# Setup of a gated cross-attention kernel: energies' input on 96 rows, other load order, gate transfers from ScalarE, Q ahead of K, first maxima between K and V

## The reference

```
xn     = layernorm(x)
Q,K,V  = xn @ Wq + bq, ctx @ Wk + bk, ctx @ Wv + bv        # 16 heads of 32
energy = mean(abs(ctxb), axis=-1);  energy /= max over keys + 1e-8
gate   = (energy > 0.1) * 0.9 + 0.1                        # one factor for each key
attn   = softmax(Q @ K.T / sqrt(32) * gate)
x      = x + tanh(g_xattn) * ((attn @ V) @ Wo + bo)
x      = x + tanh(g_ffn) * experts(layernorm(x))           # 2 shared, 16 routed, top 2
```

## Time and profile before

| what | us |
|---|---|
| median of 3 runs | 2094.84 (2093.85 to 2103.59) |
| the profiled execution | 2091.02 |
| its span | 2089.1 |
| TensorE busy in the span | 1935.3 (93%) |
| GpSimd busy | 1248.9 (60%) |
| VectorE busy | 1119.3 (54%) |
| ScalarE busy | 772.2 (37%) |
| TensorE's first matmul | 35.54 |
| first score of batch 0 | 76.36 |
| first matmul of batch 0's body | 99.76 |

### The profile page before, as it was taken

The page is one execution under the profiler, slowest core; times in us unless marked ns, Lnnn a source line. Parts: engine busy times, 40 slices in busy tenths (PEclk is TensorE's granted clock), DMA queues, the critical chain, the costliest instruction groups (busy, mean ns, idle before and its releaser), DMA issues. The chain is left out here.

```text
span 2089.1 us, 40601 instructions
## 1 busy us (share of the span) xinstructions
PE 1935.3 (93%) x12484; PEld 1503.2 (72%) x12485; DVE 1119.3 (54%) x1763; ACT 772.2 (37%) x1533; POOL 1248.9 (60%) x1398
## 2 busy tenths in 40 slices
PE   1899999999999999999999999998779799999799
PEld 1777878778787787877878777785468566666687
DVE  3465655655656565565655556565347233333476
ACT  1144444444445454444444444444222122221000
POOL 3277776777767777677776867766524233333531
PEclk9999999999999999999999999998679899999899
DMA  6646548375583745738466383664063454445864
GB/s 164 184 126 178 156 127 243 98 193 144 137 231 94 212 129 152 202 110 223 115 167 188 112 236 101 180 168 129 27 237 89 159 164 145 147 146 162 230 188 135
DMA packets 170481, 330.43 MB, mean 158 GB/s; under 512 B 20279, under 2 KB 69431, under 8 KB 169671
## 3 DMA queue, kind: packets, MB, share of 16 engines
q1 hardware_dynamic: 156724, 286.95, 48.8%
q0 software_dynamic: 10880, 33.56, 6.0%
q10 hardware_dynamic: 2832, 9.33, 1.2%
HBM read 214.17 MB, written 115.14 MB: 158 GB/s over the span
## 5 line engine op out<-in xcount | busy, mean ns | idle before, releaser
L835 DVE TENSOR_REDUCE neg_max<-score 112x1 f32<-112x750 f32 x512 | 480.4, 938 | 564.5 <-PE score L1105 563.3
L613 ACT ACTIVATE probs_t<-st 125x448 f32<-125x448 f32 x768 | 414.1, 543 | 519.4 <-PE st L1131 515.3
L470 POOL TENSOR_TENSOR acc<-acc,probs_t 125x448 f32<-125x448 f32 x256 | 309.5, 1209 | 64.8 <-ACT probs_t L613 63.0
L1069 PE MATMUL proj<-ctx_hi,weights 128*128 128x376 f32 (+1 forms) x1024 | 331.2, 349 | 10.2 <-POOL parts L425 9.7
L1131 PE MATMUL st<-q_stack,k_stack 98*125 98x224 f32 x1536 | 334.2, 301 | 6.4 <-DMA q_stack<-shift_rows 3.2
L472 POOL TENSOR_TENSOR acc<-acc,probs_t 125x448 f32<-125x448 f32 x256 | 300.1, 1172 | 20.1
L1131 PEld LDWEIGHTS st<-q_stack,k_stack 98*125 98x125 f32 x1536 | 267.8, 191 | 60.8 <-issue 28.5
L1105 PE MATMUL score<-k_stack,q_stack 96*112 96x512 f32 (+1 forms) x1024 | 284.2, 359 | 20.2 <-DVE neg_max L835 13.0
L462 POOL TENSOR_TENSOR acc<-probs_t 125x448 f32<-125x448 f32 x128 | 146.2, 1143 | 173.8 <-PE pv L1157 154.3
L1079 PE MATMUL proj<-weights,ctx_hi 128*125 128x512 f32 x768 | 246.8, 402 | 0.0
L1069 PEld LDWEIGHTS proj<-ctx_hi,weights 128*128 128x128 f32 x1024 | 192.7, 190 | 36.5 <-issue 18.2
(11 more groups left out here) (209 smaller groups left out, 2766.9 us busy)
## 6 DMA issues: line engine op xcount, KB each, us to landing
k_stack<-k_parts SPq DMA_DIRECT2D x192, 375.0 KB, 6.3
ctx_raw<-in_ctx_t SPq DMA_DIRECT2D x64, 375.0 KB, 9.9
k_parts<-k_hi SPq DMA_DIRECT2D x64, 375.0 KB, 6.6
k_parts<-k_lo SPq DMA_DIRECT2D x64, 375.0 KB, 7.2
y_slots<-y_sb SPq DMA_DIRECT2D x72, 256.0 KB, 2.9
...
```

Of the source, the lines that this page charges most:

```text
L470: nc.gpsimd.tensor_tensor(both, both, tiles(c, p, pair, 0), ALU.add).then_inc(half_added, 1)
L613: act.activation(probs_t[0:KW, (c * PHASES + p) % 2, u % HC, :], st[u % 2][0:KW, 0:2 * L], ACT.Exp)\
L835: nc.vector.tensor_reduce(neg_max[:, h // HC % 2, h % HC, t:t + 1], score[0:QW, 0:S], axis=AX.X, op=ALU.max, negate=True).then_inc(maxed, 1)
L1069: ins = nc.tensor.matmul(bank[:, 0:w], wp[:, d, c * P:(c + 1) * P], xp[:, d, at:at + w], start=(d == 0 and k == 0), stop=(d == DC - 1 and ...
```

## The change

All of it is in setup. The bodies and the experts have the same instructions in the same order.

- The energies' input is loaded as 96 rows of 125 keys, in two transfers, into a buffer that shares its place with `k_stack`, and reduced in two parts. Before it lay in V's place, as 125 rows in one transfer.
- SP's loads come in the order x, energies' input, wq, wk, context, biases; wv, wo and the small tables are issued when the gate's store has landed (`gate_out`). Q's two stores come ahead of K's first.
- ScalarE issues the energies' store and load, and no longer waits for them with its first instruction.
- GpSimd fills a quarter of the rows of ones; three transfers of ScalarE copy it to the rest. Before, GpSimd filled them in two halves.
- VectorE, not GpSimd, takes wk's remainder, in four pieces with a count each (`wk_lo_done`).
- TensorE projects Q0 and Q1 first. The first four scores stand between halves of K3a and K3b, the next four between halves of V0 and V1; before, all eight stood between halves of V0 to V3. VectorE's and ScalarE's orders follow.

```diff
-SETUP = ("XT0", "XT1", "K0a", "Q0", "K0b", "Q1", "K1a", "K1b", "K2a", "K2b", "K3a", "K3b", "V0", "V1", "V2", "V3", "SH0")
+SETUP = ("XT0", "XT1", "Q0", "Q1", "K0a", "K0b", "K1a", "K1b", "K2a", "K2b", "K3a", "K3b", "V0", "V1", "V2", "SH0", "V3")
...
+        with ExitStack() as first_use:
+            ctxb_sb = first_use.enter_context(nc.sbuf_tensor("ctxb_sb", [ROWS, B * S * NF // ROWS], F32))
         k_stack = sb("k_stack", [P, H, S], F32R)
...
+        ENERGY_ROWS = ROWS
+        ENERGY_EACH = B * S // ENERGY_ROWS
...
             load_x(0)
-            sp.dma_start(flat_v[0:ENERGY_ROWS, :],
-                         ctxb.rearrange("b s f -> (b s f)").rearrange("(p k) -> p k", p=ENERGY_ROWS)).then_inc(ctxb_in, 16)
+            ctxb_rows = ctxb.rearrange("b s f -> (b s f)").rearrange("(p k) -> p k", p=ENERGY_ROWS)
+            for i, (start, end) in enumerate(ENERGY_HALVES):
+                sp.dma_start(ctxb_sb[:, start * NF:end * NF], ctxb_rows[:, start * NF:end * NF]).then_inc(ctxb_in[i], 16)
+            sp.dma_start(wq_sb[:, :, :], wq.rearrange("(c p) n -> p c n", p=P)).then_inc(wq_in, 16)
             sp.dma_start(wk_tmp, wk.rearrange("(c p) n -> p c n", p=P)).then_inc(wk_in, 16)
             for d in range(DC):
                 load_raw(0, d)
-            sp.dma_start(wq_sb[:, :, :], wq.rearrange("(c p) n -> p c n", p=P)).then_inc(wq_in, 16)
-
-            sp.wait_ge(energy_summed, 1)
-            sp.dma_start(energy_dram.rearrange("b s -> (b s)").rearrange("(p k) -> p k", p=ENERGY_ROWS),
-                         energy_sb).then_inc(energy_out, 16)
             sp.dma_start(bq_col[:, :], bq).then_inc(bias_in, 16)
             sp.dma_start(bk_col[:, :], bk).then_inc(bias_in, 16)
+
+            sp.wait_ge(gate_out, 16)
             sp.dma_start(wv_tmp, wv.rearrange("(c p) n -> p c n", p=P)).then_inc(wv_in, 16)
...
             sp.dma_start(wo_sb[:, :, :], wo.rearrange("(c p) n -> p c n", p=P)).then_inc(tabs_in, 16)
             store_q(0, 0, -1)
-            store_k(0, 0)
-            load_stack(0, 0)
             store_q(0, 1, -1)
-            for c in (1, 2):
+            for c in range(DC - 1):
                 store_k(0, c)
                 load_stack(0, c)
...
-            pool.memset(k_stack[ROWS:SHIFTED, 0:H // 2, :].bitcast(F32), 1.0).then_inc(consts, 1)
+            pool.memset(ones_rows[:, 0:ONES_H, :], 1.0).then_inc(consts, 1)
...
             norm_factor(0)
-            pool.wait_ge(w_hi, 1)
-            remainder(wk_lo[:, :, :], wk_tmp, wk_hi[:, :, :]).then_inc(w_lo, 1)
             ctx_remainder(0, 0)
             ctx_remainder(0, 2)
-            pool.wait_ge(ctx_lo_done[0], 2)
-            pool.memset(k_stack[ROWS:SHIFTED, H // 2:H, :].bitcast(F32), 1.0).then_inc(consts, 1)
-            pool.wait_ge(consts, 8)
             for i, name in enumerate(KEYS):
                 key_low(0, name)
-                if i == 1:
-                    pool.wait_ge(w_hi, 2)
-                if 1 <= i < 1 + DC:
-                    remainder(wv_lo[:, i - 1, :], wv_tmp[:, i - 1, :], wv_hi[:, i - 1, :]).then_inc(w_lo, 1)
+                if 3 <= i < 3 + DC:
+                    d = i - 3
+                    if d == 0:
+                        pool.wait_ge(wv_hi_done, 1)
+                    remainder(wv_lo[:, d, :], wv_tmp[:, d, :], wv_hi[:, d, :]).then_inc(wv_lo_done, 1)
...
-            act.wait_ge(energy_out, 16)
-            act.dma_start(gate_b[0:B, :], energy_dram).then_inc(energy_in, 16)
+            act.wait_ge(consts, 7)
+            for i in range(1, 4):
+                act.dma_start(ones_rows[:, i * ONES_H:(i + 1) * ONES_H, :], ones_rows[:, 0:ONES_H, :]).then_inc(ones_in, 16)
...
             normalize(x_in, 0, xn_ready, 0)
             normalize(x_in, 1, xn_ready, 0)
-            ctx_high(0, 0)
-            ctx_high(0, 1)
+            act.wait_ge(energy_summed, 2)
+            act.dma_start(energy_dram.rearrange("b s -> (b s)").rearrange("(p k) -> p k", p=ENERGY_ROWS),
+                          energy_sb).then_inc(energy_out, 16)
             for t in range(QT):
                 copy_turned(-1, f"XT{t}", t)
+            ctx_high(0, 0)
+            act.wait_ge(energy_out, 16)
+            act.dma_start(gate_b[0:B, :], energy_dram).then_inc(energy_in, 16)
+            for d in range(1, DC):
+                ctx_high(0, d)
+            act.wait_ge(bias_in, 32)
+            query_high(0, 0, -1)
             act.wait_ge(gate_ready, 1)
             act.dma_start(gate_dram, gate_b[0:B, :]).then_inc(gate_out, 16)
             act.wait_ge(gate_out, 16)
             act.dma_start(gate_b[:, :], gate_dram[0:1, :].broadcast_to([P, S])).then_inc(gate_loaded, 16)
-            ctx_high(0, 2)
-            ctx_high(0, 3)
-            act.wait_ge(bias_in, 32)
-            key_high(0, "K0a", -1)
-            query_high(0, 0, -1)
-            key_high(0, "K0b", -1)
             query_high(0, 1, -1)
-            key_high(0, "K1a", -1)
+            for name in KEYS[:4]:
+                key_high(0, name, -1)
             act.wait_ge(tabs_in, TABS)
             act.activation(tanh_g[:, :], g_col[:, :], ACT.Tanh).then_inc(tanh_ready, 1)
...
-            for kt in range(4):
+            for kt in range(2):
                 copy_values(0, kt, -1)
             shift_high(0, 0, -1)
             place_shift(0, 0, -1)
+            for kt in (2, 3):
+                copy_values(0, kt, -1)
...
-            dve.wait_ge(ctxb_in, 16)
-            nc.vector.tensor_reduce(energy_sb, flat_v[0:ENERGY_ROWS, :].rearrange("p (t f) -> p t f", f=NF),
-                                    axis=AX.X, op=ALU.add, apply_absolute_value=True).then_inc(energy_summed, 1)
+            for i, (start, end) in enumerate(ENERGY_HALVES):
+                dve.wait_ge(ctxb_in[i], 16)
+                nc.vector.tensor_reduce(energy_sb[:, start:end],
+                                        ctxb_sb[:, start * NF:end * NF].rearrange("p (t f) -> p t f", f=NF),
+                                        axis=AX.X, op=ALU.add, apply_absolute_value=True).then_inc(energy_summed, 1)
             dve.wait_ge(wk_in, 16)
-            nc.vector.tensor_copy(wk_hi[:, :, :], wk_tmp).then_inc(w_hi, 1)
+            link(nc.vector.tensor_copy(wk_hi[:, :, :], wk_tmp))
+            for d in range(DC):
+                nc.vector.tensor_tensor(wk_lo[:, d, :], wk_tmp[:, d, :], wk_hi[:, d, :].bitcast(F32), ALU.subtract)\
+                    .then_inc(wk_lo_done, 1)
             ctx_remainder(0, 1)
-
...
             ctx_remainder(0, 3)
+            dve.wait_ge(bias_in, 32)
+            query_low(0, 0, -1)
+            query_low(0, 1, -1)
+            for name in KEYS[:4]:
+                gate_keys(0, name, -1)
             dve.wait_ge(wv_in, 16)
-            nc.vector.tensor_copy(wv_hi[:, :, :], wv_tmp).then_inc(w_hi, 1)
-            dve.wait_ge(bias_in, 32)
-            gate_keys(0, "K0a", -1)
-            query_low(0, 0, -1)
-            gate_keys(0, "K0b", -1)
-            query_low(0, 1, -1)
-            gate_keys(0, "K1a", -1)
-            gate_keys(0, "K1b", -1)
+            nc.vector.tensor_copy(wv_hi[:, :, :], wv_tmp).then_inc(wv_hi_done, 1)
+            gate_keys(0, "K2a", -1)
+            gate_keys(0, "K2b", -1)
             dve.wait_ge(tabs_in, TABS)
...
+            maximum(0, 0, 0)
+            maximum(0, 0, 1)
+            gate_keys(0, "K3a", -1)
+            maximum(0, 1, 0)
+            maximum(0, 1, 1)
+            gate_keys(0, "K3b", -1)
+            for h in range(2, HC):
...
                 turn_x(0, t, -1)
-            pe.wait_ge(w_lo, 1)
-            project_k(0, "K0a", -1, (0, 4))
             pe.wait_ge(wq_in, 16)
-            project_q(0, -1, (0, 8))
-            project_k(0, "K0b", -1, (0, 4))
-            project_q(1, -1, (0, 8))
+            for i in range(2):
+                project_q(i, -1, (0, 8))
+            for d in range(DC):
+                pe.wait_ge(wk_lo_done, d + 1)
+                project_k(0, "K0a", -1, (d, d + 1))
+            for name in ("K0b", "K1a", "K1b", "K2a", "K2b"):
+                project_k(0, name, -1, (0, 4))
...
-            for name in KEYS[2:]:
-                project_k(0, name, -1, (0, 4))
+            pe.wait_ge(ones_in, 16 * 3)
             score_rows(0, 0, 0)
-            pe.wait_ge(w_lo, 1 + DC)
+            project_k(0, "K3a", -1, (0, 2))
+            score_rows(0, 0, 1)
+            project_k(0, "K3a", -1, (2, 4))
+            score_rows(0, 1, 0)
+            project_k(0, "K3b", -1, (0, 2))
+            score_rows(0, 1, 1)
+            project_k(0, "K3b", -1, (2, 4))
+            score_rows(0, 2, 0)
+            pe.wait_ge(wv_lo_done, DC)
             project_v(0, -1, (0, 2))
-            score_rows(0, 0, 1)
...
-            score_rows(0, 2, 0)
             project_v(2, -1, (0, 2))
-            score_rows(0, 2, 1)
+            turn_shift(0, 0, -1)
             project_v(2, -1, (2, 4))
-            score_rows(0, 3, 0)
+            score_rows(0, 4, 0)
             project_v(3, -1, (0, 2))
-            score_rows(0, 3, 1)
```

(21 more changed lines are left out.)

13 lines of the change are left out of this document (7 added, 6 removed).

## The result

| | before | changed |
|---|---|---|
| median of 6 runs each, side by side, us | 2095.36 (2093.85 to 2103.59) | 2085.84 (2082.92 to 2088.13) |
| ratio to before, with its 95% interval | | 0.9948 (0.9931 to 0.9965) |
| the profiled execution, us | 2091.02 | 2082.92 |
| its span | 2089.1 | 2081.2 |
| T, the gate's store landed | 46.06 | 31.51 |

The account below looks back on a forecast made before the run. TensorE bounds the batches, so only setup could move: first score at 64.5 us, plus 16.3 and 8.0, puts the body at 88.8 us, 11.0 us sooner. That gives 2080.0 us profiled, 2083.8 median; range 2079 to 2088, chance 0.45.

Parts of the forecast that it names:

- The input: Setup load of the energies' input: 96 rows use all sixteen DMA engines, landed near 11 us, reduced at 13.2.
- The energies' transfers: ScalarE's store and load of the energies: 5.5 us each, load landing at 26 us, giving T = 31.
- Behind T: Setup after the gate's store: Q0's store lands at T + 13.0 behind wv to wo, K0b's low part ends T + 18.0.
- From K0b to the first score: K0b's low part to the stack's landing: 15.5 us as before, first score at T + 33.5 = 64.5 us.
- The scores: First score to the shift's issue, with K3 and half of V2 between: 16.3 us, against 15.4 before.
- The shift: Shift rows' transfer before batch 0's body: 8.0 us to landing, mostly covered by V3 and four scores.
- Rival (c): Shift rows queue behind batch 1's loads: 5.7 us over the forecast, or 2096.6 us at the slow end; chance 0.06.
- The sum: Batch 0's body starts at 88.8 us against 99.76, 11.0 us less; batch 0's own 123.8 us kept.
- (a): Rival: ScalarE's transfers don't stand behind SP's; T = 27.5, body at 83, 2078 us; chance 0.23.
- (b): Rival: the gain goes into queues; T = 35, body at 99.2, 0.6 us gained, 2094 us; chance 0.22.
- (d): Rival: 96 rows land no sooner than 125; T = 44, added wait offsets it, 2094 to 2097 us; chance 0.04.
- the wait added behind T: SP's wait for the gate's store before wv to wo, with Q0's store and all keys queued behind: 3.9 us.

Follow-up runs that it names:

- e2: The changed kernel with the energies' input back on 125 rows in V's place; one run, 2093.19 us.
- e1: The kernel before with only the energies' input on 96 rows in k_stack's place; ratio 0.9948 to before.
- e8: e6 with VectorE forming the gate between the halves of wk's remainder, the context's remainders behind it; ratio 0.9921 to before.
- e5: The changed kernel without SP's wait for the gate's store ahead of wv to wo; ratio 0.9910 to before.
- e3: The changed kernel with Q0's store issued ahead of SP's wait for the gate's store; ratio 0.9929 to before.
- e6: e5 with wv's high and low parts made ahead of the keys; ratio 0.9916 to before.
- e11: The changed kernel again, unaltered, on the second chip; ratio 0.9953 to before.
- e7: e6 with K3a and K3b ahead of the first score, as before the change; ratio 0.9916 to before.
- e12: e1 again, the 96 rows alone on the kernel before, on the second chip; ratio 0.9952 to before.

## Why the forecast held, step by step

**The input.** Forecast 11 us and summed at 13.2; measured 10.54 and 12.79. Between x, there at 4.81 us, and 10.54 us the 1500 KB make 262 KB/us, where five engines at the prediction's 15.7 KB/us would give 79. It is the landing that shows this. The DMA share of 1.00 from 6 to 10 us is no sign by itself, since before, while the input was late, it was 0.99 in the same stretch, with other loads in flight:

```profile
6.00:10.00 4.00, 0.00 (x0) 0.00 (x0) 0.90 (x1) 0.00 (x0) 2.99 (x9) 1.00 0.99 214
```

The Trainium skill's rule (DMA: Bandwidth & Descriptors, "Why a DMA increments its semaphore by 16 and not by 1") had this step right for both row counts: 10.54 us with 96 rows, and with 125 rows in e2 the last part is back at 24.25 us. No cost of the copies of the ones shows: e1, which has none, had its input at 11.28 us.

**The energies' transfers.** Store forecast 5.5 us, measured 5.7. The load was forecast at 5.5, landing at 26; it took 3.6 and had landed at 23.5, but VectorE took it at 26.65 only, held by four wk remainders of 5.67 us in all and one of the context. I had put these down as over by then. Two errors cancelled, 2.5 us on the load and 3.1 us on VectorE, so it is luck that T came at 31.51 us against 31. That wk's remainder was moved to VectorE has a price, and e8 shows it: 1.8 us of T.

**Behind T.** This is the term that was mis-sized. I wrote T + 12.3 from the rows, took T + 13.0 and kept T + 15 as the bound; it was T + 16.2, outside the bound. By parts: wv to wo were issued in 3.6 us (4.1 in the sum), Q0's four stores in 5.5 us (2.5), and they landed 7.1 us after the last issue (5.7). The mechanism is the one forecast, q queued behind wo, but I took the four issues at their price on free queues. SP's own rows show that an issue right behind wv and wo takes up to 2.03 us, and the window that I used for wo's 11.1 us held the same sign before: wo's issue took 1.57 us. In e5, with the weights gone early, the same store is issued in 2.7 us and lands 5.9 us later. The low part of K0b ended at T + 20.9 instead of T + 18.0.

**From K0b to the first score.** Forecast 15.5 us, measured 13.8 (52.42 to 66.24). The load of the stack was issued at 58.70 us, 6.3 us behind K0b's low part, where before it was 7.6 us (60.15 to 67.72, behind Q0's store and its load). Sum of both: first score at T + 34.7 instead of T + 33.5.

**The scores.** Forecast 16.3 us to the shift's issue, measured 17.1. The second to fourth scores came at distances of 2.66 and 1.86 us instead of 1.6. TensorE had stood still for 2.74 us before the first score; in the stretch from 68 to 70 us its granted clock is 0.50, the lower level of 1.2 GHz, and it works all of it. e3, e5, e6 and e8, whose first score waited for its stack too, show the same level in their first scores. e11, the same kernel as the changed one, waited 2.23 us and stayed at 1.00, as did e2. And in e7 the first score waited for no stack, yet the clock was 0.50 from 74 to 77 us. What decides on the fall is open here; that it is not the change itself is shown by e11.

**The shift.** Its landing was forecast at 8.0 us, mostly covered; by the body it had been 7.1 us, and TensorE waited 0.79 us. Rival (c), the shift behind batch 1's loads, was not met: batch 1's x was issued at 79.83 us, ahead of it, and did no harm.

**The sum.** 88.8 us forecast, 90.37 measured, 9.4 us gained instead of 11.0. T took 0.5 of the difference, T to the first score 1.2, the scores 0.8; the shift gave 0.9 back. The rest of the kernel, from the body's start to the span's end, was 1990.8 us against 1989.3.

**The rivals.** (a) needed T at 27.5 us and short transfers. The transfers of ScalarE took longer beside SP's, 5.7 us against 1.7 to 1.9 on idle queues (the gate's store; the energies' load in e2). I had written there that by the Trainium skill's rule of turns between queues (DMA: Bandwidth & Descriptors, "Queues, rings and completion order") the old load of 8.3 us must have stood in part on the five late engines. e1 shows that it didn't need to: with 96 rows and no late engine, but wv and wo in flight, the same load took 7.6 us, and 7.8 in e12. In e5, where it is issued 7.8 us behind wv instead of 4.5, it was 4.9 us (5.1 in e6, 5.0 in e8). Why it is shorter there was not separated. (b) had the gain go into queues; that is what happened to 4.4 us of it (34.73 against 30.30 behind T), not to all. (d) is refuted by 10.54 us. e2 is the kernel that (d) describes, and its T was 40.41 us and not 44: the chain from the input didn't stay as it was, since the energies' load took 1.9 us.

What the forecast lacked is the comparison that e1 makes. It gave one number for the whole change and didn't say that the input alone would give it: the wait added behind T was in the sum at 3.9 us, and it never priced what the other parts win at T, which is 2.4 us (e1 against the changed kernel). So it couldn't see that they lose more than they win.
